# Moving DMA issues between the queues of a fused attention and expert layer, with the expert weights cast once into DRAM

## The reference

```python
qkv = x @ W_qkv + b_qkv                      # 1024 x 3072
attn = softmax(q @ k.T / 32)                 # one head, 4096 x 4096
x = layernorm(x + (attn @ v) @ W_out + b_out)
grouped = x.reshape(256, 16, 1024)           # groups of 16 tokens
logits = grouped @ controller + tie          # 64 experts
perm = (logits == logits.max(over the 16 tokens))
sel = one token for each group and expert
inner = relu(sel @ f1[expert] + bias)        # 1024 -> 64
inter = inner @ f2[expert]                   # 64 -> 1024
out = inter summed back to the token that was chosen
x = layernorm(x + out)
```

## Time and profile before

| | us |
|---|---|
| median of 2 runs | 2381.38 (2379.11 to 2383.66) |
| the profiled execution | 2400.24 |
| its span, slowest core (1) | 2398.7 |
| spans of the eight cores | 2361.4 to 2398.7 |
| projections | 0 to 480 |
| attention | 480 to 1636 |
| routing | 1636 to 1716 |
| four rounds of gather and experts | 1716 to 2190 |
| combination | 2190 to 2399 |

### The profile page before, as it was taken

How to read it: one execution, slowest core, us unless ns; L and a number is a source line. 1 busy time by engine, 2 the same in 40 slices (tenths; PEclk the granted TensorE clock), 3 DMA queues, 4 the chain that set the end, 5 groups by cost and what they waited for, 6 DMA issues and landing times.

```text
span 2398.7 us, 35921 instructions; the slowest of 8 cores (2361.4 to 2398.7 us)
## 1 busy us (share of the span) xinstructions
PE 1972.7 (82%) x13216; PEld 1311.9 (55%) x13216; DVE 517.8 (22%) x840; ACT 553.6 (23%) x1121; POOL 266.2 (11%) x457
## 2 busy tenths in 40 slices
PE   0498899989999999999999999993577777676564
PEld 0143344477777887777887777881344343332222
DVE  0010001101111011111101111101514343333555
ACT  0122222122222222222222222220243333332000
POOL 2000000000000000000000000000133333233442
PEclk9999988899999999999999999996655655555777
DMA  9714411030000100010000100007297969698997
GB/s 136 102 36 87 81 44 44 18 62 28 28 27 14 36 19 27 27 41 24 14 19 27 41 28 27 6 14 138 67 175 193 169 188 163 183 163 201 309 306 253
DMA packets 227974, 213.83 MB, mean 89 GB/s; under 512 B 147360, under 2 KB 171936, under 8 KB 227488
## 3 DMA queue, kind: packets, MB, share of 16 engines
q0 software_dynamic: 100688, 109.21, 23.6%
q10 hardware_dynamic: 36864, 67.13, 7.7%
q1 hardware_dynamic: 90256, 35.20, 6.9%
HBM read 161.28 MB, written 75.50 MB: 99 GB/s over the span
## 4 chain that ended last, share of the span: by engine, by line
PE 66%; DMA 21%; DVE 5%; SPq 3%; issue 3%; ACT 1%; POOL 1%; DVEq 1%; ACTq 0%; POOLq 0%
PE pb L127 57%; PE pb L124 8%; DMA intersp<-arenaB 8%; DMA arenaC<-hsp 7%; SPq L113 3%; DVE arenaB L134 2%; DMA qsp<-qstage 1%; DMA arenaA<-xbf 1%; DMA xbf<-x 1%; DMA arenaB<-f 1%; POOL arenaB L113 1%; DVE arenaA L134 1%; DVE bnbuf L136 1%; DVE arenaA L136 1%; DVE arenaC L136 1%
## 5 line engine op out<-in xcount | busy, mean ns | idle before, releaser
L127 PE MATMUL pb<-arenaA,arenaB 128*128 128x256 bf16 (+1 forms) x4032 | 578.4, 288 | 14.5 <-DMA arenaA<-qsp 6.3
L127 PE MATMUL pb<-arenaA 128*128 128x512 bf16 x1856 | 486.1, 398 | 117.5 <-DMA arenaA<-xbf 93.2
L127 PE MATMUL pb<-arenaA,arenaC 128*128 128x256 bf16 x4120 | 540.5, 275 | 24.3 <-DVE arenaA L134 19.0
L127 PEld LDWEIGHTS pb<-arenaA,arenaB 128*128 128x128 bf16 (+1 forms) x4032 | 413.6, 105 | 120.7 <-issue 67.6
L127 PEld LDWEIGHTS pb<-arenaA,arenaC 128*128 128x128 bf16 x4120 | 403.1, 98 | 78.8 <-issue 31.3
L134 ACT ACTIVATE arenaA<-pb,smalls 128x256 bf16<-128x256 f32 x512 | 240.8, 473 | 756.1 <-PE pb L124 722.5
L127 PEld LDWEIGHTS pb<-arenaA 128*128 128x128 bf16 x1856 | 185.3, 101 | 369.3 <-issue 241.1
L127 PE MATMUL pb<-arenaB 128*128 128x512 bf16 (+1 forms) x384 | 166.2, 525 | 144.1 <-DMA arenaC<-hsp 72.1
L136 DVE RECIPROCAL arenaF<-pb 128x256 f32<-128x256 f32 x16 | 28.1, 1758 | 880.0 <-PE pb L124 880.0
L127 PEld LDWEIGHTS pb<-arenaB 128*128 128x128 bf16 (+1 forms) x384 | 41.4, 113 | 258.0 <-issue 246.5
L124 PE MATMUL pb<-arenaA,arenaB 128*128 128x256 bf16 (+1 forms) x576 | 165.5, 287 | 0.0
(11 more groups left out here) (53 smaller groups left out, 1100.8 us busy)
## 6 DMA issues: line engine op xcount, KB each, us to landing
arenaC<-hsp POOLq DMA_DIRECT2D x160, 256.0 KB, 3.7
intersp<-arenaB ACTq DMA_DIRECT2D x128, 256.0 KB, 2.9
arenaB<-intersp POOLq DMA_DIRECT2D x128, 256.0 KB, 8.1
arenaB<-f POOLq DMA_DIRECT2D x128, 128.0 KB, 5.1
y<-arenaF ACTq DMA_DIRECT2D x32, 512.0 KB, 8.5
xbf<-x POOLq DMA_DIRECT2D x4, 2048.0 KB, 21.4
qsp<-qstage ACTq DMA_DIRECT2D x64, 128.0 KB, 2.2
arenaA<-qsp SPq DMA_DIRECT2D x16, 512.0 KB, 3.9
```

The lines of the kernel that those rows point to most:

```text
L127: e.matmul(o, l, r, start=st, stop=sp))
```

## The change

Two DRAM tensors are added, `f1b` and `f2b`, that hold f1 and f2 in bfloat16. GpSimd casts into them by eight DMAs (2 MB written each), issued right behind the loads of `W_out` at the beginning of the attention. The loads of the experts' weights read these, and are issued by ScalarE. The loads of h in the gather go from GpSimd to SP. The stores of `intersp` go from ScalarE to GpSimd, with their waits. In the combination two of the four `intersp` pieces go to SP, two stay with GpSimd, and the tile of h goes to ScalarE. Waits for the semaphores follow the DMAs. The rest of the kernel is as before.

```diff
+    f1b_d = nc.dram_tensor("f1b", [D, ES * FW], BF16, kind=SCR).ap()
+    f2b_d = nc.dram_tensor("f2b", [ES, FW * D], BF16, kind=SCR).ap()
@@ after the loads of W_out @@
+    for i in range(4):
+        fc1_done = dma("gpsimd", "fc1", f1b_d[i * 256:(i + 1) * 256, :],
+                       f1_d[i * 256:(i + 1) * 256, :])
+    for i in range(4):
+        fc2_done = dma("gpsimd", "fc2", f2b_d[i * 16:(i + 1) * 16, :],
+                       f2_d[i * 16:(i + 1) * 16, :])
@@ load_ht @@
-        wait("gpsimd", "sT", ht_free_T[slot])
-        ht_ld[slot] = dma("gpsimd", "hg%d" % slot,
+        wait("sync", "sT", ht_free_T[slot])
+        ht_ld[slot] = dma("sync", "hg%d" % slot,
                           ht4(slot), hsp_d[t * 128:(t + 1) * 128, :])
@@ load_fw @@
-            wait("gpsimd", "sT", max(f1_free_T[slot_t], inner_free_T[slot_t]))
+            wait("scalar", "sT", max(f1_free_T[slot_t], inner_free_T[slot_t]))
-            f1_src = f1_d[:, es_t * FW:(es_t + 1) * FW].rearrange(
+            f1_src = f1b_d[:, es_t * FW:(es_t + 1) * FW].rearrange(
                 "(c p) f -> p c f", p=128)
-            f1_ld[slot_t] = dma("gpsimd", "f1%d" % slot_t, f1_dst, f1_src)
+            f1_ld[slot_t] = dma("scalar", "f1%d" % slot_t, f1_dst, f1_src)
-            f2_src = f2_d[es_t:es_t + 1, :].rearrange("a (f d) -> (a f) d", f=FW)
-            f2_ld[slot_t] = dma("gpsimd", "f2%d" % slot_t, f2_dst, f2_src)
+            f2_src = f2b_d[es_t:es_t + 1, :].rearrange("a (f d) -> (a f) d", f=FW)
+            f2_ld[slot_t] = dma("scalar", "f2%d" % slot_t, f2_dst, f2_src)
@@ the store of intersp @@
-                wait("scalar", "sV", iv)
-                wait("scalar", "sC", ic)
+                wait("gpsimd", "sV", iv)
+                wait("gpsimd", "sC", ic)
                 istg_free[istg] = dma(
-                    "scalar", ichan,
+                    "gpsimd", ichan,
@@ load_it @@
+        wait("sync", "sT", it_free_T[slot])
         wait("gpsimd", "sT", it_free_T[slot])
         for c in range(4):
+            if c < 2:
+                ig_ld[slot] = dma("sync", "ig%d" % slot, dst, src_ap)
+            else:
+                ib_ld[slot] = dma("gpsimd", "ib%d" % slot, dst, src_ap)
         hslot = t % 4
-        wait("gpsimd", "sT", ht2_free[hslot])
-        hld_t[hslot] = dma("gpsimd", "hg%d" % hslot, ht4(hslot),
+        wait("scalar", "sT", ht2_free[hslot])
+        hld_t[hslot] = dma("scalar", "hh%d" % hslot, ht4(hslot),
                            hsp_d[t * 128:(t + 1) * 128, :])
```

More of the change, by code:

```diff
@@ L271, in build_nc @@
     bout_done = dma("sync", "bout", FP[:, 1024:2048], bout_t_d)
+    fc1_done = 0
+    for i in range(4):
+        fc1_done = dma("gpsimd", "fc1", f1b_d[i * 256:(i + 1) * 256, :],
+                       f1_d[i * 256:(i + 1) * 256, :])
+    fc2_done = 0
+    for i in range(4):
+        fc2_done = dma("gpsimd", "fc2", f2b_d[i * 16:(i + 1) * 16, :],
+                       f2_d[i * 16:(i + 1) * 16, :])
     qload = [0] * (NQ + 2)
@@ L629, in build_nc @@
     ht_ld = [0, 0, 0, 0]
-    wait("gpsimd", "h0", P_cnt["h0"])
-    wait("gpsimd", "h1", P_cnt["h1"])
+    wait("sync", "h0", P_cnt["h0"])
+    wait("sync", "h1", P_cnt["h1"])
     f1_free_T = [logits_T_done] * 4
@@ L702, in load_fw @@
             slot_t = esl_t % 4
-            wait("gpsimd", "sT", max(f1_free_T[slot_t], inner_free_T[slot_t]))
+            wait("scalar", "sT", max(f1_free_T[slot_t], inner_free_T[slot_t]))
             f1_dst = B[:, F1B + slot_t * 512: F1B + (slot_t + 1) * 512].rearrange(
                 "p (c f) -> p c f", c=NCH)
-            f1_src = f1_d[:, es_t * FW:(es_t + 1) * FW].rearrange(
+            f1_src = f1b_d[:, es_t * FW:(es_t + 1) * FW].rearrange(
                 "(c p) f -> p c f", p=128)
-            f1_ld[slot_t] = dma("gpsimd", "f1%d" % slot_t, f1_dst, f1_src)
+            f1_ld[slot_t] = dma("scalar", "f1%d" % slot_t, f1_dst, f1_src)
             f2_dst = B[0:64, F2B + slot_t * 1024: F2B + (slot_t + 1) * 1024]
-            f2_src = f2_d[es_t:es_t + 1, :].rearrange("a (f d) -> (a f) d", f=FW)
-            f2_ld[slot_t] = dma("gpsimd", "f2%d" % slot_t, f2_dst, f2_src)
+            f2_src = f2b_d[es_t:es_t + 1, :].rearrange("a (f d) -> (a f) d", f=FW)
+            f2_ld[slot_t] = dma("scalar", "f2%d" % slot_t, f2_dst, f2_src)
+        if ec == 0:
+            wait("scalar", "fc1", fc1_done)
+            wait("scalar", "fc2", fc2_done)
         load_fw(0)
@@ L810, in build_nc @@
     ig_ld = [0, 0, 0]
+    ib_ld = [0, 0, 0]
     hld_t = [0, 0, 0, 0]
@@ L815, in build_nc @@
     wait("gpsimd", "sT", p4_T_done)
+    wait("sync", "is0", P_cnt["is0"])
+    wait("sync", "is1", P_cnt["is1"])
+    wait("sync", "sT", p4_T_done)
+    wait("scalar", "sT", p4_T_done)
     def pe_pt(t):
@@ L842, in load_it @@
             src_ap = intersp_d[16 * c:16 * (c + 1), t * 8:(t + 1) * 8, :]
-            ig_ld[slot] = dma("gpsimd", "ig%d" % slot,
-                              B[:, ITO + slot * 4096 + c * 1024:
-                                ITO + slot * 4096 + (c + 1) * 1024], src_ap)
+            dst = B[:, ITO + slot * 4096 + c * 1024:
+                    ITO + slot * 4096 + (c + 1) * 1024]
+            if c < 2:
+                ig_ld[slot] = dma("sync", "ig%d" % slot, dst, src_ap)
+            else:
+                ib_ld[slot] = dma("gpsimd", "ib%d" % slot, dst, src_ap)
         hslot = t % 4
-        wait("gpsimd", "sT", ht2_free[hslot])
-        hld_t[hslot] = dma("gpsimd", "hg%d" % hslot, ht4(hslot),
+        wait("scalar", "sT", ht2_free[hslot])
+        hld_t[hslot] = dma("scalar", "hh%d" % hslot, ht4(hslot),
                            hsp_d[t * 128:(t + 1) * 128, :])
@@ L863, in build_nc @@
         wait("tensor", "ig%d" % slot, ig_ld[slot])
-        wait("tensor", "hg%d" % hslot, hld_t[hslot])
+        wait("tensor", "ib%d" % slot, ib_ld[slot])
+        wait("tensor", "hh%d" % hslot, hld_t[hslot])
         b0 = (t % 2) * 2
```

## The result

The changed kernel takes 2444.8 us in the median (11 runs), the kernel before 2387.7 us in the same comparison (10 runs). The ratio is 1.0253, 95% interval 1.0228 to 1.0278: 60 us slower. Some executions have a lower granted clock on some or all of their cores and take longer; the medians hold them, the ratios leave them out, and of casts_fours only the four undisturbed cores are read. The forecast was slower too, but by 22 us. The time is inside the range; the size is not right, and the stages show that the reasons were not right either.

A forecast was written before the change was run, and what follows sets the result against it. It took the ring of `intersp` stores, not TensorE, to bound the experts. Terms +64 - 16 - 12 + 15 - 26 + 0 + 0 - 3 = +22 us, applied to the median of 2381, gave 2403 us, range 2345 to 2460.

The forecast's parts named there:

- The casts: Attention: eight casts, some 155 us, stay under the cover of the blocks; 0, bounds 0 to +17 us.
- the casts reaching the attention's critical loads: Attention: named as one way the prediction would be wrong; no size given.
- The stores on GpSimd: Expert parts: slower reaction and transfer add 1.0 us to each of 64 experts; +64 us, bounds +32 to +90.
- The ring's 4.5 us: Expert parts: an expert's period is its `intersp` store's landing, some 3.5 us, plus 0.96 us of eviction and hand-overs.
- The weights in bfloat16: Expert parts: weights hold the engines for less time, so stores land 0.3 us sooner for 52 experts; -16 us, bounds 0 and -40.
- The late landings at a round's end: Expert parts: next round's loads of h, issued from SP, no longer delay a store; three rounds, -12 us, bounds -12 and 0.
- The first weights of a round: Start of each expert part: weights issued behind ScalarE's last eviction come 3.7 us later; +15 us, bounds +6 and +24.
- The gather: Four gathers: loads of h from SP take a tile from 1.2 to 1.0 us; -26 us, bounds -38 and -10.
- The combination: Combination: fewer issues on POOL against h standing behind y, engines at 0.93; 0, with -14 and +20 us.
- Rival C: Combination turns on the tile of h behind y: +0.6 us a tile, +20 over the forecast, 2423 us; chance 0.13.
- The routing: Routing: four loads of h no longer stand beside the five transposes; -3 us, 0 to -6.
- Rival B: Expert parts: POOL stores slow beside the weights, landing above 4.3 us, +1.4 us an expert; +92, 2473 us; chance 0.17.

The follow-up runs named there:

- casts_fours: Kernel before plus the eight casts in two bursts of four, behind attention blocks 0 and 6, read by nothing: attention 1158.2 to 1173.4 us on cores 4 to 7.
- w_pool: Changed kernel with one cast to a block, `intersp` stores on ScalarE, bfloat16 weights from GpSimd, the combination's tile of h from SP: ratio 0.9753 to before.
- gather_sp: Kernel before with only the loads of h in the gather moved from GpSimd to SP: ratio 0.9987.
- w_sp: Changed kernel with one cast to a block, `intersp` stores on ScalarE, bfloat16 weights and the combination's tile of h from SP: ratio 0.9788 to before.
- comb_only: Kernel before with the change's moves in the combination alone, tile of h from ScalarE behind the store of y: ratio 1.0095, combination 212.1 us.
- comb_h_sp: Kernel before with two of four `intersp` pieces and the tile of h from SP in the combination: ratio 1.0033, combination 201.6 us.
- stage4: Kernel before with four staging slots for the stores of `intersp` in place of two: ratio 0.9757, expert parts 248.4 us.

## Why the prediction was right or wrong

**The casts (0 forecast, +42 measured): the step that failed.** I priced a landing beside them at 17 us from one store of Q, which stood beside one cast, and then set that against the cover of a block. What a landing costs is its own packets for an engine times the length of a cast's packet, until the burst ends: 110.3 us for a load of Q, 42 and 76 us for the two stores of h. The row with 17.31 us was right and the use of it was wrong. The cast of x was over after some 20 us, so that nothing beside it could take longer, and the store of Q landed when it ended. That store has a quarter of the bytes of a load of Q and, with 8 packets for an engine in place of 64, an eighth of its packets. With eight casts in a row, 155 us, that ceiling was gone. I bounded the term by two landings of 17 us, and the bound was below the result. The prediction named this way of being wrong, the casts reaching the attention's critical loads, but gave it no price.

**The stores on GpSimd (+64 forecast, +44 measured).** The mechanism held: the reaction of 0.48 us is in the chain, and the landing is 0.9 us longer where I took 0.5. The term was too large for the other reason, TensorE's own time of 3.8 us an expert at the lower clock, which I had not set as a floor. My rows held it: 59.32 us for sixteen experts, 3.7 us each, while the ring with a landing of 2.16 us is 3.1. The ring's 4.5 us for every expert was also read too simply: the chain follows the late stores, and the page of the kernel before has a median landing of 2.9 us, not 3.5:

```profile
intersp<-arenaB ACTq DMA_DIRECT2D x128, 256.0 KB, 2.9
```

**The weights in bfloat16 (-16 forecast, -43 measured).** The mechanism was right and the size wrong: this is the term of the experts that was sized too small. 1.2 us an expert and not 2.4 is what they hold the engines for, and more of the stores' wait beside them went than a fifth: the median landing is 2.5 us in w_pool and 3.7 in gather_sp, the two kernels that the 43 us come from.

**The late landings at a round's end (-12 forecast, nothing measured)**, in gather_sp. The landings of 7 us are gone (the longest of core 0 is 6.7), but the expert parts are not shorter. The last stores of rounds 0 to 2, which had landed in 2.0 to 3.1 us but for the very last, take up to 5.8 on that core. What makes them slower, no run shows.

**The first weights of a round (+15 forecast, +9 measured).** The wait is the forecast one, 4.67 us in round 1 against 4 to 5; w_sp gives back 9 us. The forecast had no such wait in the kernel before; two of its rounds do wait for the weights, for 1.8 and 1.9 us on core 1.

**The gather (-26 forecast, -4 measured).** I took 2.8 us for a load from SP, from the quiet 2.6; under the gather's own traffic it takes 3.5, and the sooner reaction is used up by that.

**The combination (0 forecast, +13 measured).** Rival C, with the right mechanism: I had the two ends within 0.1 us of each other in the sum and put them down as equal, and h does land as late as forecast, 14.4 us after TensorE's end. The step that failed is to take the same end for the same time: before, that landing was late because the engines were full, and now because h is issued late, with the engines idle for a part of it (91% in comb_only against 98% in comb_h_sp).

**The routing (-3 forecast, -2 measured)**, which is within the spread of the cores of the kernel before, 128.0 to 137.3 us.

Taken together, the forecast's +22 came from +36 in the experts and -11 in the gathers, which turned out as +2 and +1, and the measured +60 came nearly all from two places where it had 0. That the experts came out at +2 is two misses of opposite sign, +44 and -43, and not a forecast that held. Rival B, slow stores, is refuted: the landing was 3.1 us, not above 4.3. Of the signs that I named, "the attention's blocks unchanged at 71 us in spite of 155 us of casts" failed at once, and so did three others: the landing of 3.1 us is below the 3.5 to 4.2 named as right, an expert part is 75.5 us and not 76 to 84, a gather 44.5 us and not 34 to 40.

## What to carry to other kernels

A transfer is not free because the engines are idle at the time: ask for how long it keeps others from landing, and hold that against the shortest cover of what is already in flight; a burst of long-row copies should be cut in shorter rows or dealt out, one to a block, and then cost nothing here that could be measured. Put what stands in a ring of two buffers on the queue that reacts soonest, or add buffers until nobody waits for it; two more staging slots were worth 2.4% here, more than any one move between queues in the kernel before. Do not put a load that is needed next behind a store in the stream of an engine that computes.

## What the runs showed of the hardware

The packets of a cast from DRAM to DRAM with rows of 16384 numbers are 32 KB long, 4.8 us each, and the engines give each queue one packet in turn (97 of each of three queues in 25 us). A plain load that takes 3.9 us alone took 110.3 us beside a row of them; with packets of 4 KB, 52.3 us. Reading 1024 pieces of 128 bytes in bfloat16 held the engines for 1.2 us an expert, together with f2, where the casting loads of 256 bytes held them for 2.8. A store of 256 KB landed in 3.1 us from GpSimd and in 2.2 from ScalarE, in kernels that differ in nothing else. The shares for which the queues hold the engines don't add up to a floor: they came to 115% in stage4, and the 4.4 us an expert of such a sum to 3.9 measured.
